# A fused twelve-layer kernel: equal mask indices share one sum, and the side work of four feed-forward units stands in other chunks

## What is computed

```python
x = x + 0.5 * _L0_ffn_ref(_layernorm(x), w_gate, w_up, w_down)   # silu(gate) * up, then down
x = x + _L0_attn_ref(_layernorm(x), ...)                         # recurrent step
x = x + 0.5 * _L0_ffn_ref(_layernorm(x), w_gate, w_up, w_down)
x = x + 0.5 * _L1_ffn_ref(...)
...
deltas = softmax(expert_atom_weights) @ atoms          # 8 x 2048
weighted = deltas * sigmoid(importance)
rows, cols = mask_idx // H, mask_idx % H               # 2048 places in a 256 x 256 matrix
xg = xt[:, cols]
contrib = segment_sum((xg * vals).T, rows)             # equal places add up
out = xt @ W.T + contrib.T
```

## Time and profile before

| | us |
|---|---|
| median of 3 runs | 1278.54 (1276.63 to 1281.75) |
| the profiled execution | 1268.16 |
| its span | 1266.4 |
| TensorE busy in the span | 1089.8 (86%) |
| VectorE busy | 853.4 (67%) |
| ScalarE busy | 610.6 (48%) |
| GpSimd busy | 556.8 (44%) |

### The profile page before, as it was taken

How to read it: one execution, slowest core, us unless ns; L and a number is a source line. 1 busy time by engine, 2 the same in 40 slices (tenths; PEclk the granted TensorE clock), 3 DMA queues, 4 the chain that set the end, 5 groups by cost and what they waited for, 6 DMA issues and landing times.

```text
span 1266.4 us, 21759 instructions
## 1 busy us (share of the span) xinstructions
PE 1089.8 (86%) x6561; PEld 936.7 (74%) x6561; DVE 853.4 (67%) x2319; ACT 610.6 (48%) x1435; POOL 556.8 (44%) x666
## 2 busy tenths in 40 slices
PE   5886557999779999978879988993799998999996
PEld 4765446877667779866667776992699997899995
DVE  5577678468987867658867867565665655666666
ACT  2454844221112345557847863550455554555552
POOL 5555716753346450235524428223435352444430
PEclk9898878999889999989989997996899999999998
DMA  5113421240004023422511122342101011010101
GB/s 174 60 62 127 159 89 50 88 125 20 1 1 181 0 97 113 127 65 56 169 46 44 34 76 86 116 128 71 48 29 41 33 41 34 26 45 30 43 7 34
DMA packets 48452, 87.86 MB, mean 69 GB/s; under 512 B 9649, under 2 KB 28465, under 8 KB 47921
## 3 DMA queue, kind: packets, MB, share of 16 engines
q1 hardware_dynamic: 41232, 70.17, 17.5%
q0 software_dynamic: 5120, 13.83, 3.6%
q10 hardware_dynamic: 2016, 2.83, 0.6%
HBM read 61.24 MB, written 19.27 MB: 64 GB/s over the span
## 4 chain that ended last, share of the span: by engine, by line
PE 54%; DVE 18%; ACT 6%; issue 4%; POOL 2%; DMA 1%; SPq 1%; DVEq 0%; POOLq 0%; ACTq 0%
PE ps L282 16%; PE ps L283 15%; PE ps L284 15%; PE ps L1818 4%; DVE a_ptl L1842 3%; ACT a_p L1787 2%; DVE a_p L1779 2%; ACT a_pth L1834 2%; DVE x L1560 1%; PE ps L856 1%; PE ps L1588 1%; PE ps L415 1%; PE ps L875 1%; POOL raw L1238 1%; DVE m_b L772 1%
## 5 line engine op out<-in xcount | busy, mean ns | idle before, releaser
L1805 POOL TENSOR_SCALAR a_p<-a_p,small 128x128 f32<-128x128 f32 (+3 forms) x256 | 131.8, 532 | 234.2 <-DVE small L1796 234.2
L1787 ACT ACTIVATE a_p<-a_p,small 128x128 f32<-128x128 f32 (+3 forms) x256 | 141.6, 554 | 76.5 <-DVE small L1779 76.0
L1842 DVE TENSOR_TENSOR a_ptl<-ps,a_pth 128x384 fp32r<-128x384 f32 (+1 forms) x192 | 106.7, 597 | 62.5 <-ACT a_pth L1834 62.3
L282 PE MATMUL ps<-xh,wh 128*128 128x512 f32 x304 | 125.9, 414 | 7.3 <-DVE xl L443 4.4
L283 PE MATMUL ps<-xl,wh 128*128 128x512 f32 x304 | 122.8, 404 | 0.0
L284 PE MATMUL ps<-xh,wl 128*128 128x512 f32 x304 | 122.2, 402 | 0.0
L1834 ACT ACTIVATE a_pth<-ps 128x384 fp32r<-128x384 f32 (+1 forms) x192 | 90.4, 524 | 57.6 <-PE ps L1818 57.6
L1779 DVE CUSTOM_DVE_ANT_0 a_p<-ps,maskrow 128x128 f32<-128x128 f32 (+3 forms) x256 | 111.7, 484 | 6.8 <-PE ps L1768 3.8
L391 POOL TENSOR_TENSOR rstd<-veps,nhalf 128x4 f32<-128x4 f32 x24 | 25.1, 1048 | 161.0 <-DVE veps L335 161.0
L476 POOL TENSOR_TENSOR wl<-raw,wh 128x1024 fp32r<-128x1024 f32 (+1 forms) x66 | 91.1, 1380 | 5.5
L1818 PE MATMUL ps<-ident,a_p 128*128 128x128 f32 x640 | 85.3, 281 | 8.3 <-POOL a_p L1805 4.4
...
## 6 DMA issues: line engine op xcount, KB each, us to landing
...
```

The source lines that it names most:

```text
L282: pe.matmul(o, l[0], r[0], start=start, stop=False, skip_group_check=True)
L1787: s.activation(p[:, par, P_AT[i]:P_AT[i + 1]], p[:, par, P_AT[i]:P_AT[i + 1]], ACT.Exp, bias=h_nmx[:, par, i:i + 1], scale=scale, accum_ou ...
L1805: g.tensor_scalar(pp, pp, h_inv[:, par, i:i + 1], 1.0, ALU.mult, ALU.mult).then_inc(sem("at_norm"), 1)
L1842: ins = v.tensor_tensor(dst, ps[:, bank, 0:cols], f32(hi), ALU.subtract)
```

## The change

The triangle products go. A value now goes to its place in the table unless an equal index stands in a later tile; equal indices of one tile all carry the same sum and all write it to the same place. So `d_tri`, its one-column matmul, the subtraction of its count and the memset of the column of ones leave the program, TensorE and ScalarE wait for the compare (`d_eqs`), and the row sum of tile k starts one tile later (the last tile needs none: its count is set to zero).

In the four units, `act_delta` comes behind the hi copy of its chunk and no longer ahead of it. In unit 0 the Exps go from chunk 3 to chunk 2, the softplus from chunks 2 and 3 to chunks 4 and 5, the constants from chunk 5 to chunk 4. Unit 5 becomes one of the written-out units; the quarters go to chunks 1, 3 and 5 of unit 4 and chunk 1 of unit 5, the ternary weights to chunks 3, 4 and 6 of unit 5. `pe_delta_end` waits for the first `d_wb` copy in unit 0, for the summed values (`d_cmb`) in unit 1 and for nothing in unit 4.

```diff
                 s.activation(ffn_s[:, p, :], ps[:, 2 + p, :], ACT.Silu).then_inc(sem("ffn_silu"), 1)
-                if u in DELTA_UNITS:
-                    act_delta(s, u, j)
                 s.wait_ge(sem("ffn_h"), f0 + 1 + j)
...
                 s.activation(ffn_hh[:, p, :], ffn_hf[:, p, :], ACT.Copy).then_inc(sem("ffn_hi"), 1)
+                if u in DELTA_UNITS:
+                    act_delta(s, u, j)
...
-        DELTA_UNITS = (0, 1, 4)
+        DELTA_UNITS = (0, 1, 4, 5)
+        QUARTERS = ((4, 1), (4, 3), (4, 5), (5, 1))
...
-            if u == 0 and j == 3:
+            if u == 0 and j == 5:
                 act_softplus(s)
+            if u == 0 and j == 2:
                 s.wait_ge(sem("d_max"), 1)
...
                 for k in EQ_SLOTS[j - 1]:
-                    s.wait_ge(sem("d_eqtri"), k + 1)
+                    if k == NK - 1:
+                        continue
+                    s.wait_ge(sem("d_eqs"), k + 1)
                     if k >= 1:
                         s.wait_ge(sem("d_rows"), k)
-                    s.activation(d_junk[:, 0:NS - k * P], d_eq[:, k % 3, k * P:NS], ACT.Copy,
+                    s.activation(d_junk[:, 0:NS - (k + 1) * P], d_eq[:, k % 3, (k + 1) * P:NS], ACT.Copy,
                                  accum_out=d_later[:, k:k + 1]).then_inc(sem("d_rows"), 1)
-            if u == 4 and j < 4:
+            if (u, j) in QUARTERS:
...
-                    pe.wait_ge(sem("d_eqtri"), k + 1)
+                    pe.wait_ge(sem("d_eqs"), k + 1)
                     for m in range(k, NK):
-                        pe.matmul(o[:, m, 0:24], d_eq[:, k % 3, m * P:(m + 1) * P], d_wb[:, k, 0:24],
-                                  start=(k == 0 and m == 0), stop=False, skip_group_check=True)
-                    pe.matmul(o[:, k, 24:25], d_tri[:, k % 2, :], d_wb[:, k, 24:25], start=False, stop=(k == NK - 1),
-                              skip_group_check=True).then_inc(sem("d_comb"), 1)
-            if u == 4 and j == 5:
+                        last = pe.matmul(o[:, m, 0:24], d_eq[:, k % 3, m * P:(m + 1) * P], d_wb[:, k, 0:24],
+                                         start=(k == 0 and m == 0), stop=(k == NK - 1), skip_group_check=True)
+                    last.then_inc(sem("d_comb"), 1)
+            if u == 5 and j == 6:
...
             if u == 0:
-                pe.wait_ge(sem("d_wb"), 4)
+                pe.wait_ge(sem("d_wb"), 1)
             elif u == 1:
-                pe.wait_ge(sem("d_dest"), 1)
-            else:
+                pe.wait_ge(sem("d_cmb"), 3)
+            elif u == 5:
                 pe.wait_ge(sem("q3_ready"), 2)
...
-                    then(v.tensor_scalar(d_eq[:, k % 3, k * P:NS], d_row[:, k * P:NS], d_colf[:, k:k + 1], None,
-                                         ALU.is_equal))
-                    settled()
-                    if k >= 2:
-                        v.wait_ge(sem("d_comb"), k - 1)
-                    v.tensor_tensor(d_tri[:, k % 2, :], d_eq[:, k % 3, k * P:(k + 1) * P], trib[:, :], ALU.mult)\
-                        .then_inc(sem("d_eqtri"), 1)
+                    v.tensor_scalar(d_eq[:, k % 3, k * P:NS], d_row[:, k * P:NS], d_colf[:, k:k + 1], None,
+                                    ALU.is_equal).then_inc(sem("d_eqs"), 1)
...
-                v.wait_ge(sem("d_rows"), NK)
-                then(v.tensor_tensor(d_dup, d_later, o[:, :, 24], ALU.subtract))
+                then(v.memset(d_later[:, NK - 1:NK], 0.0))
```

More of the change, by code:

```diff
@@ L106 @@
           "m_tabs": ("d_mx0", 1), "m_in0": ("x_in0", 16), "m_in1": ("x_in1", 16), "m_in2": ("ident_in", 16),
-          "m_in3": ("d_zeroed", 64), "m_out0": ("d_eqtri", 16), "m_out1": ("d_rows", 16), "m_raw0": ("d_wb", 4),
+          "m_in3": ("d_zeroed", 64), "m_out0": ("d_eqs", 16), "m_out1": ("d_rows", 15), "m_raw0": ("d_wb", 3),
           "m_raw1": ("sp_2", 9), "wo_raw": ("sp_1", 1), "wo_hi": ("sp_abs", 1), "wo_lo": ("sp_y", 1),
@@ L2302, in act_delta @@
                 for k in EQ_SLOTS[j - 1]:
-                    s.wait_ge(sem("d_eqtri"), k + 1)
+                    if k == NK - 1:
+                        continue
+                    s.wait_ge(sem("d_eqs"), k + 1)
                     if k >= 1:
                         s.wait_ge(sem("d_rows"), k)
-                    s.activation(d_junk[:, 0:NS - k * P], d_eq[:, k % 3, k * P:NS], ACT.Copy,
+                    s.activation(d_junk[:, 0:NS - (k + 1) * P], d_eq[:, k % 3, (k + 1) * P:NS], ACT.Copy,
                                  accum_out=d_later[:, k:k + 1]).then_inc(sem("d_rows"), 1)
-            if u == 4 and j < 4:
+            if (u, j) in QUARTERS:
+                q = QUARTERS.index((u, j))
                 s.wait_ge(sem("m_xzero"), 16 * 8)
-                s.wait_ge(sem(f"d_back{j // 2}"), 16)
-                src, hi, _ = delta_quarter(j)
+                s.wait_ge(sem(f"d_back{q // 2}"), 16)
+                src, hi, _ = delta_quarter(q)
                 s.activation(hi, src, ACT.Copy).then_inc(sem("delta_hi"), 1)
@@ L2392, in dve_delta @@
                 then(v.tensor_scalar(d_col[:, 2, :], d_col[:, 0, :], 8, None, ALU.logical_shift_right))
-            if u == 0 and j == 2:
-                dve_softplus(v)
+            if u == 0 and j == 4:
+                dve_softplus_start(v)
+                dve_consts(v)
             if u == 0 and j == 5:
-                dve_consts(v)
+                dve_softplus_rest(v)
             if u == 0 and j == 3:
@@ L2416, in dve_delta @@
                 wk = d_wt.rearrange("p (k e) -> p k e", e=E)
-                v.memset(d_wb[:, :, 24:25], 1.0).then_inc(sem("d_wb"), 1)
                 v.tensor_copy(d_wb[:, :, 0:8], wk).then_inc(sem("d_wb"), 1)
-                v.wait_ge(sem("d_wb"), 2)
+                v.wait_ge(sem("d_wb"), 1)
                 then(v.tensor_tensor(d_r1.rearrange("p (k e) -> p k e", e=E), wk, d_wb[:, :, 0:8], ALU.subtract))
@@ L2423, in dve_delta @@
                 v.tensor_copy(d_wb[:, :, 8:16], r1).then_inc(sem("d_wb"), 1)
-                v.wait_ge(sem("d_wb"), 3)
+                v.wait_ge(sem("d_wb"), 2)
                 then(v.tensor_tensor(r2, r1, d_wb[:, :, 8:16], ALU.subtract))
@@ L2444, in dve_delta @@
                 v.tensor_copy(cmb, o[:, :, 0:8]).then_inc(sem("d_cmb"), 1)
-                v.wait_ge(sem("d_rows"), NK)
-                then(v.tensor_tensor(d_dup, d_later, o[:, :, 24], ALU.subtract))
+                then(v.memset(d_later[:, NK - 1:NK], 0.0))
                 v.wait_ge(sem("d_cmb"), 1)
                 v.tensor_tensor(cmb, cmb, o[:, :, 8:16], ALU.add).then_inc(sem("d_cmb"), 1)
+                v.wait_ge(sem("d_rows"), NK - 1)
                 settled()
-                then(v.tensor_scalar(d_dup, d_dup, 1.0, None, ALU.min))
+                then(v.tensor_scalar(d_dup, d_later, 1.0, None, ALU.min))
                 then(v.tensor_tensor(d_pos, d_pos, d_dest, ALU.subtract))
@@ L2459, in dve_delta @@
                 v.tensor_copy(d_desti[:, :], d_dest).then_inc(sem("d_dest"), 1)
-            if u == 4 and j < 4:
-                src, hi, lo = delta_quarter(j)
-                v.wait_ge(sem("delta_hi"), j + 1)
+            if (u, j) in QUARTERS:
+                q = QUARTERS.index((u, j))
+                src, hi, lo = delta_quarter(q)
+                v.wait_ge(sem("delta_hi"), q + 1)
                 v.tensor_tensor(lo, src, f32(hi), ALU.subtract).then_inc(sem("delta_lo"), 1)
-            if u == 4 and j == 3:
+            if u == 5 and j == 3:
                 v.wait_ge(sem("d_in_q3"), 16)
@@ L2473, in dve_delta @@
                 then(v.tensor_scalar(d_thr[:, 2:4], d_thr[:, 0:2], 1.0 / D, 0.7, ALU.mult, ALU.mult))
-            if u == 4 and j == 4:
+            if u == 5 and j == 4:
                 settled()
@@ L2541, in dve_consts, with dve_softplus_start @@
             v.wait_ge(sem("const_in"), 16 * CONSTS)
-        def dve_softplus(v):
+        def dve_softplus_start(v):
             v.wait_ge(sem("const_in"), 16 * CONSTS)
@@ L2548, in dve_softplus, with dve_softplus_rest @@
             v.tensor_tensor(sp_abs, p, sp_t, ALU.max).then_inc(sem("sp_abs"), 1)
+        def dve_softplus_rest(v):
+            p = rgp[:, :, 7]
             v.wait_ge(sem("sp_y"), 1)
```

## The result

The changed kernel takes 1263.58 us (median of four runs, 1260.9 to 1264.76), the kernel before 1277.59 in the runs beside it (1276.09 to 1281.75): ratio 0.9882, 95% interval 0.9853 to 0.9911, 14.0 us faster. The forecast was 1261, the range 1253 to 1271. The time is right. The table shows that, against the second trace of before, 5.2 of the 17.4 us come from a stage that the change does not touch (against the first trace none do), and that the four units it does touch gave less than forecast.

The account below looks back on a forecast made before the run. TensorE, busy 86% of the span, was taken as the bound, waiting for side work in four units. Gains 3.0 + 9.8 + 7.1 - 2.3 = 17.6 us, scaled to 17.7 off 1278.54, gave 1261; range 1253 to 1271.

Parts of the forecast that it names:

- The scaling: Whole kernel: 17.6 us off the profiled 1268.16 becomes 17.7 off the median 1278.54, which is 0.8% higher.
- Unit 0: Feed-forward unit 0: earlier Exps let the 32 small matmuls start 2.0 to 3.9 us earlier; 3.0 gained.
- Unit 1: Feed-forward unit 1: 17.0 us leave VectorE's chain, less 4.2 and 3.0 given back; 9.8 gained, ends 3.7 and 15.0.
- Term (a): Unit 1: compares meet GpSimd's instructions where the products did and take back 4.2 us, bound 0 to 8.4.
- Term (b): Unit 1: row sums behind hi hold compares and Silu of chunk 6; 3.0 us lost, ends 0 and 4.9.
- Term (c): Unit 1's end: transposes, last product and unit 2 queue behind d_cmb in place of d_desti; counted as 0.
- Unit 4: Feed-forward unit 4: 9.75 us excess over unit 5, less 1.4 and 1.2 that stay; 7.1 gained, ends 3.2 and 9.75.
- Unit 5: Feed-forward unit 5: 1.4 us for its quarter and 0.9 for ternary work; 2.3 lost, ends 0.4 and 5.5.
- The clock rival: Units 1, 4 and 5: spread short waits hold TensorE at 1.2 GHz; 8.5 us slower, 1287; chance 0.05.
- The first rival: Unit 1: compares inherit port waits and later sums cost as before; gains only 3.7, total 1267; chance 0.20.
- the second's 15.0: Unit 1: rival that every TensorE wait goes, 15.0 us; with other units 26.4, total 1252; chance 0.15.
- the port rule in full: Unit 1: VectorE's waits for GpSimd pass to the compares, up to all 8.4 us; sign: compare mean over 1.3.

Follow-up runs that it names:

- the second trace of before: The kernel before, unchanged, profiled a second time: profiled execution 1280.34 us, timed median 1280.18 us.
- u5_unroll: The kernel before with unit 5's middle chunks written out and no longer a loop, no work moved: 1271.9 us, ratio 0.9947 to before.
- smt_first: The changed kernel with VectorE's copy of the transposed softmax ahead of softplus steps and constants in unit 0: 1259.74 us, ratio 0.9836 to before.
- rg_pieces: The changed kernel with GpSimd's splits of the recurrent step's weights, at unit 1's end, cut into 256-column pieces: 1260.41 us, ratio 0.9856 to before.
- u1_only: The kernel before with unit 1's part of the change alone: 1274.38 us, ratio 0.9949 to before.
- q_pieces: The changed kernel with VectorE's quarter of delta cut from one 1024-column instruction into four of 256: 1265.9 us, ratio 0.9883 to before.

## Why the prediction was right, and where it was not

**The total.** The four units were to give 17.6 us and gave 11.5 (0.0 + 8.5 + 5.8 - 2.8). The missing 6.1 was filled by 5.9 from elsewhere, the mixture layer and the attention unit behind it above all. The prediction held that nothing in the change touches the rest of the span. That step failed: no instruction there changed, but its length did, and u5_unroll gets some 6.6 us from writing unit 5 out alone. That the total came within 3 us of 1261 is luck to that extent. The four units by themselves would have led to 1277.6 - 11.5 = 1266, still inside the range. (The pair of traces differs by 17.4, the medians by 14.0: the second trace of before, 1280.34, stands 2.8 above the median of 1277.59, the trace of the changed kernel 0.5 below its own.) The range was given as 1253 to 1271, 1 us inside the 1252 and 1272 of its own sums; nothing hangs on it.

**The scaling.** 17.6 off 1268.16 was carried over to the median of 1278.54 in proportion, as if every stage were 0.8% longer. The second trace shows that the difference sits in the mixture layer (6.7), unit 4 (1.3), unit 0 (0.9) and a few us behind. It did no harm to the sum, but that trace hid the stage in which the gain would come.

**Unit 0 (3.0, measured 0.0).** The failed step is the start of the small matmuls, "2.0 to 3.9 earlier". The transpose came at 38.14, not 37.2, mostly since lo of chunk 3 took 1.42 and not 0.69. The softplus steps and the constants took 41.12 to 44.33, 3.2 us; the sum allowed 0.3 + 0.91 + 1.9 = 3.1, which is close. But chunk 4 of VectorE ended at 41.1, not 40.2, and so the matmuls started 0.93 earlier only, behind a wait of 1.8. The clock fell at 47.1, while they ran: they took 4.68 and not the 3.74 of the earlier trace rows, so the 0.93 was gone at their end. What the clock costs was nowhere in the sum for this unit. smt_first shows both: with the wait gone and the low stretch half as long, 3.5 us go.

**Unit 1 (9.8, measured 8.5).** Right in size, and by other terms. Term (a), the port waits that the compares inherit, was 4.2 and is 3.1 (18.5 - 15.4). Its reason is shown by rg_pieces: with GpSimd's instructions cut, 2.7 of the 3.1 are gone (15.8). The Trainium skill (SBUF — State Buffer, section "SBUF: two separate sides") says that the pair of ports that VectorE and GpSimd share is held for a whole instruction and the loser fully blocks; 2.88 beside a split of 2.35 and 0.92 beside pieces agree. By its rule in full, as the prediction read it, all 8.4 would have passed on; 3.1 did. Term (b), the later sums, failed: counted as 4.9 - 3.0 = 1.9 gained, it gave nothing that can be seen (50.6 with the early sums, 51.1 to 52.2 with the later ones). The 4.2 us of VectorE's waits for hi that went were not on TensorE's path. So what is left of the edit, the products gone and the sums one tile shorter, gave some 10 in the traces (60.5 to 60.7 down to 50.6), not 17.0 - 4.9 - 4.2 = 7.9. Term (c), nothing at the end, held: 3.1 for d_cmb where 2.6 was for d_desti.

**Unit 4 (7.1, measured 5.8 against the second trace, 4.5 against the first).** VectorE's wait for lo at chunk 1 went nearly away, but GpSimd's splits, held behind each quarter, were priced at 0.6 each for two quarters and cost TensorE 3.7 in four waits. That term was mis-sized. The old unit itself is no fixed quantity: 46.33 to 49.13 in five traces with TensorE idle for 7.2 to 7.4 in each, by the clock. In the changed kernel 3.9 are idle, and only the first 3 us, to 180.24, run at 0.50, a stretch that began ahead of the unit. u5_unroll's and u1_only's unit 4:

```profile
185.44:231.77 46.33, 39.06 (x205) 32.49 (x205) 30.79 (x43) 21.69 (x27) 29.45 (x31) 0.93 0.28 95
```
```profile
176.53:225.66 49.13, 41.87 (x204) 34.80 (x205) 30.93 (x43) 22.32 (x27) 29.52 (x31) 0.86 0.26 90
```

**Unit 5 (2.3 lost, measured 2.8)** and **the rivals.** Unit 5 came as forecast, clock 1.00. The clock rival fell: the granted clocks of units 1, 4 and 5 are 0.91, 0.96 and 1.00, against 0.92, 0.93 and 1.00 in the first trace of before and 0.86, 0.89 and 1.00 in the second. The first rival's 3.7 for unit 1 and the second's 15.0 fell too: unit 1 gave 8.5, and of TensorE's 15.0 us of waits there 8.8 are left (5.7 + 3.1). The compares' mean of 1.18 us is under the 1.3 that the prediction named for the port rule in full. Of the rival in which the port keeps all waits, q_pieces shows the mechanism in another place: what leaves GpSimd's account comes back on VectorE's.

**What stays open** is why the mixture layer takes 97 in three of four traces of kernels with the old units 4 and 5 and the loop, 90.6 in the fourth, and 91.5 to 94.0 in all ten of the others. Neither the loop nor the place of the quarters nor the place of the code decides alone, and each trace is one execution.
